# A decoder layer on one core: the score maxima of each batch element packed into one transposed block, and the decay matrix of the last two batch pairs, not only the last, built on TensorE

## The reference

```python
# 1: attention with 16 heads of 8 features, with a gate tau per query and a term delta per key
Q, K = projections of x through a linear map and a convolution of 3 taps;  V = linear(x)
scores = (Q K^T / sqrt(8)) * tau + delta
x = layernorm(x + linear(softmax(scores) V))
# 2: mLSTM cell, 4 heads of 32 features, causal
F = cumsum(log_sigmoid(fg));  log_D[s,t] = F[s] - F[t] + ig[t] for t <= s, else -inf
m = max_t log_D;  C = (q k^T / sqrt(32)) * exp(log_D - m)
hst = C / (max(|sum C|, exp(-m)) + 1e-6) @ v;  per-head normalisation
x = layernorm(x + hst)
# 3: x and the weight rounded to an fp6 grid in blocks of 32 with a scale each, matmul, bias
x = layernorm(x + xd @ wd^T + bias)
```

## Time and profile before

| | us |
|---|---|
| median of 3 runs | 238.55 (237.43 to 240.87) |
| profiled execution | 238.0 |
| its span, first to last instruction | 236.3 |
| granted TensorE clock, mean | 0.949 of 2.4 GHz |

### The profile page before, as it was taken

One profiled execution on the slowest core, in us unless ns is written; L12 is line 12 of the kernel. 1 busy time (PEld: TensorE's weight loads), 2 busy tenths in 40 slices (PEclk: granted clock), 3 DMA queues, 4 the chain that ended last, 5 costly groups with the idle time before them and its releaser, 6 DMA issues. The chain is left out here.

```text
span 236.3 us, 5909 instructions
## 1 busy us (share of the span) xinstructions
PE 208.4 (88%) x2217; PEld 132.0 (56%) x2217; DVE 154.1 (65%) x354; ACT 134.2 (57%) x346; POOL 132.0 (56%) x239
## 2 busy tenths in 40 slices
PE   1799889699999999899888899789889969699895
PEld 1676454244566455566546567366648756276552
DVE  4587889959444553557647779966684475556871
ACT  2632867556854643673763768757776465515332
POOL 7994629691232192581695848862781757523520
PEclk9997999979999999999999999999997967899799
DMA  5822110000000000202002003003002003000001
GB/s 145 206 37 78 47 47 0 1 0 3 0 3 3 0 3 1 92 3 81 11 1 94 3 1 115 0 25 97 23 0 67 28 8 103 3 22 1 22 1 47
DMA packets 10220, 8.40 MB, mean 36 GB/s; under 512 B 1872, under 2 KB 9264, under 8 KB 10192
## 3 DMA queue, kind: packets, MB, share of 16 engines
q1 hardware_dynamic: 8816, 7.83, 11.2%
q0 software_dynamic: 512, 0.18, 0.7%
q10 hardware_dynamic: 864, 0.01, 0.2%
HBM read 6.94 MB, written 1.08 MB: 34 GB/s over the span
## 5 line engine op out<-in xcount | busy, mean ns | idle before, releaser
L996 DVE TENSOR_REDUCE nm<-score 128x8 f32<-128x1024 f32 x32 | 39.1, 1223 | 22.0 <-PE score L740 22.0
L511 ACT ACTIVATE prob<-score 128x1024 f32<-128x1024 f32 x32 | 32.6, 1021 | 21.2 <-PE score L755 21.0
L740 PE MATMUL score<-km,qf 32*128 32x512 f32 x128 | 35.0, 640 | 0.8 <-ACT prob L511 0.7
L750 PE MATMUL score<-qm,kf 32*128 32x512 f32 x128 | 35.0, 639 | 0.8 <-DVE nm L996 0.8
L775 PE MATMUL pvb<-ones 128*128 128x512 bf16 x80 | 23.5, 436 | 0.0
L359 POOL CAST nmx<-nm 128x16 bf16<-128x16 f32 x16 | 4.1, 254 | 30.4 <-DVE nm L996 30.4
L381 POOL TENSOR_TENSOR u<-u,maskb 128x1024 f32<-128x1024 f32 x7 | 16.5, 2358 | 7.2 <-DMA u<-gates_out 7.2
L768 PE MATMUL pvb<-prob,vz 128*32 128x128 f32 x512 | 17.4, 277 | 2.2 <-ACT prob L511 2.2
L859 PEld LDWEIGHTS qkb<-ctm,cc 128*128 128x128 f32 x128 | 15.3, 194 | 4.3 <-issue 2.2
L768 PE MATMUL pvb<-prob,ez 128*32 128x128 f32 x512 | 16.9, 273 | 0.0
L859 PE MATMUL qkb<-ctm,cc 128*128 128x33 f32 x128 | 15.7, 278 | 1.3 <-DVE cc L1069 0.8
(11 more groups left out here) (248 smaller groups left out, 485.8 us busy)
## 6 DMA issues: line engine op xcount, KB each, us to landing
u<-gates_out SPq DMA_DIRECT2D x7, 512.0 KB, 3.7
xt<-in_x_dram SPq DMA_DIRECT2D x4, 256.0 KB, 4.3
cin<-in_ctx_dram SPq DMA_DIRECT2D x4, 256.0 KB, 3.4
out_dram<-th SPq DMA_DIRECT2D x8, 128.0 KB, 1.9
ck<-in_L_attn_convk_w_dram SPq DMA_DIRECT2D x1, 192.0 KB, 3.6
cq<-in_L_attn_convq_w_dram SPq DMA_DIRECT2D x1, 192.0 KB, 3.9
pk<-in_L_attn_kproj_w_dram SPq DMA_DIRECT2D x1, 128.0 KB, 2.9
pq<-in_L_attn_qproj_w_dram SPq DMA_DIRECT2D x1, 128.0 KB, 3.4
```

The costliest lines, as they stand in the source:

```text
L511: nc.scalar.activation(prob[:, n % 2, 2 * h:2 * h + 2, :].rearrange("p g s -> p (g s)"), sc[:, 1024 * h:1024 * (h + 1)], ACT.Exp, scale=0. ...
L740: ins = mm(sc[:, 512 * q:512 * (q + 1)], qf[r, n, :], km[r, n % (2 * CB)].rearrange("p j s -> p (j s)"), start=True, stop=True)
L750: mm(sc[:, 512 * q:512 * (q + 1)], kf[r, m, :], qm[r, m % (2 * CB)].rearrange("p j s -> p (j s)"), start=True, stop=False)
L996: nc.vector.tensor_reduce(nm[:, n % RING, 8 * h:8 * (h + 1)], sc[:, 1024 * h:1024 * (h + 1)].rearrange("p (h s) -> p h s", h=8), AX_X, ALU ...
```

## The change

- `nmx` is one block of 128 columns per element: column 32 g + 4 s + j holds part s of the maximum of head 4 g + j. One transpose instead of four, and `nmT` is 128 x 128. POOL's split has the same four instructions.
- Since the four j now share their columns, the right one must be picked: new tensors `msel` and `sel`, made once on DVE in step `vzero`. `sel[:, j, :]` is one in the rows whose index is j modulo 4. Form B adds the maxima with 8 matmuls of 32 x 128 columns (j outside, the two banks of the half inside) instead of 2 of 32 x 512.
- `LATE` is 6: pairs 6 and 7 have their decay matrix built on PE and their row-wise steps on DVE; the `dec_done` counts follow, and `x2b` on POOL, with the late steps' indices, comes twice.
- `warm` issues one matmul per step, 80 steps.
- `PLACES` is new throughout.

The diff, cut to its core:

```diff
-LATE = PAIRS - 1
+LATE = PAIRS - 2
...
-        mcol = sb("mcol", [P, J]);
+        mcol = sb("mcol", [P, J]); msel = sb("msel", [P, J]); sel = sb("sel", [P, J, P], BF16)
...
-        nmx = sb("nmx", [P, RING, J * (S + 1)], BF16)
-        nmT = sb("nmT", [P, RING, J * S], BF16)
+        nmx = sb("nmx", [P, RING, P], BF16)
+        nmT = sb("nmT", [P, RING, S], BF16)
...
-                    x3 = nmx[:, n % RING, :].rearrange("p (j c) -> p j c", j=J)
-                    hi, mid, lo = (x3[:, :, J * s:J * s + 3 * 32 + 1:32] for s in range(3))
+                    x3 = nmx[:, n % RING, :].rearrange("p (g c) -> p g c", g=G)
+                    hi, mid, lo = (x3[:, :, J * s:J * (s + 1)] for s in range(3))
...
-                    nc.scalar.activation(nmT[:, n % RING, :], trb[:, 0:J * S // 2].bitcast(BF16), ACT.Copy).then_inc(nmT_sb, 1)
+                    nc.scalar.activation(nmT[:, n % RING, :], trb[:, 0:S // 2].bitcast(BF16), ACT.Copy).then_inc(nmT_sb, 1)
...
                         pe.wait_ge(nmT_sb, m + 1)
-                        for q in (2 - 2 * h, 3 - 2 * h):
-                            r = slice(32 * q, 32 * (q + 1))
-                            ins = mm(sc[:, 512 * q:512 * (q + 1)], ones[r, :], nmT[r, m % RING, :], start=False, stop=True)
+                        if k == 0:
+                            pe.wait_ge(vzero, 1)
+                        for j in range(J):
+                            for q in (2 - 2 * h, 3 - 2 * h):
+                                r = slice(32 * q, 32 * (q + 1))
+                                ins = mm(sc[:, 512 * q + S * j:512 * q + S * (j + 1)], sel[r, j, :], nmT[r, m % RING, :], start=False, stop=(j == J - 1))
                         ins.then_inc(b_ready, 1)
...
                     pe.wait_ge(*pved)
-                    for k in range(2):
-                        mm(pvb[:], ones[:], ones[:].unsqueeze(1).to_broadcast([P, 512 // P, P]), start=True, stop=True)
+                    mm(pvb[:], ones[:], ones[:].unsqueeze(1).to_broadcast([P, 512 // P, P]), start=True, stop=True)
...
-                    for j in range(J):
-                        ins = nc.tensor.transpose(trb[:, 0:J * S // 2].bitcast(BF16)[:, S * j:S * (j + 1)],
-                                                  nmx[:, n % RING, S * j:S * (j + 1)], identb[:])
-                    ins.then_inc(nmT_ps, 1)
+                    nc.tensor.transpose(trb[:, 0:S // 2].bitcast(BF16), nmx[:, n % RING, :], identb[:]).then_inc(nmT_ps, 1)
...
-                    nc.vector.memset(vz[:], 0.0).then_inc(vzero, 1)
+                    nc.vector.memset(vz[:], 0.0)
+                    link(nc.vector.tensor_reduce(msel[:], ident[:].rearrange("p (a j) -> p j a", j=J), AX_X, ALU.max))
+                    nc.vector.tensor_copy(sel[:], msel[:].unsqueeze(2).to_broadcast([P, J, P])).then_inc(vzero, 1)
...
-                    dve.wait_ge(dec_done, p + 1)
+                    dve.wait_ge(dec_done, p + 1 + max(0, p - LATE))
...
-                                dve.wait_ge(dec_done, p + 2)
+                                dve.wait_ge(dec_done, 2 * p + 2 - LATE)
```

More of the change, by code:

```diff
@@ L40 @@
 PHASES = 2 * (B + LAG) + 1
-LATE = PAIRS - 1
+LATE = PAIRS - 2
 PLACES = {
[10 rows of a table removed]
[L55 to L62, removed]
[7 rows of a table removed]
[L70 to L75, removed]
[6 rows of a table removed]
-    "mkk": (0, 1, 2, 3, 17, 18, 19, 23, 36, 37, 40, 41, 49, 51, 52, 53), "res": (4, 5, 6, 12),
-    "mkq": (7, 8, 10, 11, 14, 15, 20, 22, 38, 39, 42, 43, 57, 58, 59, 60), "gcb": (9, 13, 21, 24, 26, 27, 31, 32),
[3 rows of a table removed]
-    "out": (75, 81, 85, 96, 102, 107, 110), "x2b": (109,), "spread": (0, 1, 2, 3, 6, 8, 9),
-    "store": (4, 5, 7, 10, 11, 12, 13, 14),
[11 rows of a table added]
+    "hst": (84, 94, 123, 131, 159, 171, 195, 215), "xdT": (96, 118, 137, 146, 190, 197, 223, 251),
+    "ffn": (99, 126, 141, 150, 194, 211, 227, 255),
+    "warm": (175, 176, 178, 179, 180, 181, 183, 184, 185, 186, 188, 189, 191, 192, 193, 198, 199, 200, 201, 202, 203, 204, 205, 206, 207, 208, 209, 210, 212, 213, 214, 216, 217, 218, 219, 220, 221, 222, 224, 225, 226, 228, 229, 230, 231, 232, 233, 234, 235, 236, 237, 238, 239, 240, 241, 242, 243, 244, 245, 246, 247, 248, 249, 250, 252, 253, 254, 256, 257, 258, 259, 260, 261, 262, 263, 264, 265, 266, 267, 268),
+    "vzero": (0,), "wab_o": (1,), "tapt": (2, 4, 15, 16, 30, 31, 37, 40), "wm_o": (3, 5), "ww_o": (6, 12),
+    "tapd": (7, 11, 17, 18, 27, 28, 35, 36), "wt_o": (8,), "wd": (9,), "fb": (10,), "bias": (13,),
+    "ko": (14, 21, 33, 39), "qo": (19, 23, 34, 41), "wo_o": (20,), "qs": (22, 32, 38, 44), "wr_o": (24,),
+    "max": (25, 29, 42, 43, 46, 48, 49, 51, 54, 56, 59, 62, 65, 67, 73, 77, 81, 87, 89, 93, 98, 103, 105, 107, 114, 120, 123, 127, 130, 136, 137, 147),
[8 rows of a table added]
+    "idt": (1, 2, 11, 12, 27, 29, 39, 41), "idd": (3, 4, 14, 16, 23, 25, 37, 38),
+    "get": (5, 6, 17, 18, 32, 33, 44, 45), "ged": (8, 10, 20, 21, 26, 30, 40, 43), "cxe": (9, 49, 56, 63),
+    "th": (13, 31, 42, 47), "dt": (15, 22, 36, 46), "cme": (24, 28, 51, 54, 57, 60, 71, 74),
+    "nmTe": (34, 52, 58, 65, 73, 79, 86, 97, 106, 114, 120, 127, 140, 147, 157, 164), "edx": (48,),
+    "exps": (50, 53, 55, 59, 62, 64, 69, 72, 77, 78, 83, 88, 92, 93, 102, 105, 110, 111, 117, 119, 122, 130, 136, 139, 143, 146, 150, 152, 162, 166, 167, 172),
[6 rows of a table added]
+    "mkk": (0, 1, 2, 3, 4, 6, 7, 15, 32, 33, 35, 36, 55, 56, 57, 59),
+    "mkq": (5, 11, 13, 14, 18, 19, 20, 21, 39, 40, 41, 43, 61, 62, 65, 66), "res": (8, 9, 10, 22),
+    "gcb": (12, 16, 26, 27, 29, 30, 38, 42),
[3 rows of a table added]
+    "x2b": (103, 105), "spread": (0, 1, 3, 4, 6, 8), "store": (2, 5, 7, 9, 10, 11, 12, 13),
@@ L354, in _ @@
                         pool.wait_ge(nmT_ps, n - RING + 1)
-                    v = nm[:, n % RING, :].rearrange("p (g j) -> p j g", j=J)
-                    rv = nr[:].rearrange("p (j g) -> p j g", j=J)
-                    x3 = nmx[:, n % RING, :].rearrange("p (j c) -> p j c", j=J)
-                    hi, mid, lo = (x3[:, :, J * s:J * s + 3 * 32 + 1:32] for s in range(3))
+                    v = nm[:, n % RING, :].rearrange("p (g j) -> p g j", j=J)
+                    rv = nr[:].rearrange("p (g j) -> p g j", j=J)
+                    x3 = nmx[:, n % RING, :].rearrange("p (g c) -> p g c", g=G)
+                    hi, mid, lo = (x3[:, :, J * s:J * (s + 1)] for s in range(3))
                     link(nc.gpsimd.tensor_copy(hi, v))
@@ L406, in _ @@
                     nc.gpsimd.tensor_tensor(x2b[:], x2[:], fbc[:].unsqueeze(1).to_broadcast([P, 2, D]), ALU.add).then_inc(x2b_done, 1)
-                if due("x2b", t) is not None:
-                    pool.wait_ge(x2_done, LATE + 1)
-                    pool.wait_ge(z3_done, LATE)
+                if (i := due("x2b", t)) is not None:
+                    p = LATE + i
+                    pool.wait_ge(x2_done, p + 1)
+                    pool.wait_ge(z3_done, p)
                     nc.gpsimd.tensor_tensor(x2b[:], x2[:], fbc[:].unsqueeze(1).to_broadcast([P, 2, D]), ALU.add).then_inc(x2b_done, 1)
@@ L1094, in _ @@
                                             ALU.mult).then_inc(t2_done, 1)
-                if due("z2l", t) is not None:
-                    dve.wait_ge(t2_done, LATE + 1)
-                    hf = hc[:, LATE % 2].rearrange("p (b h) d -> p b (h d)", b=2)
+                if (i := due("z2l", t)) is not None:
+                    p = LATE + i
+                    dve.wait_ge(t2_done, p + 1)
+                    hf = hc[:, p % 2].rearrange("p (b h) d -> p b (h d)", b=2)
                     link(nc.vector.tensor_tensor(hf, hf, rows[:, 0, :].unsqueeze(1).to_broadcast([P, 2, D]), ALU.mult))
-                    dve.wait_ge(x2_done, LATE)
-                    nc.vector.tensor_tensor(z2[:], hf, x1[:, LATE % 3, :, 0:D], ALU.add).then_inc(z2_done, 1)
-                if due("x2l", t) is not None:
-                    dve.wait_ge(rs2_done, LATE + 1)
-                    dve.wait_ge(qa_done, LATE)
+                    dve.wait_ge(x2_done, p)
+                    nc.vector.tensor_tensor(z2[:], hf, x1[:, p % 3, :, 0:D], ALU.add).then_inc(z2_done, 1)
+                if (i := due("x2l", t)) is not None:
+                    p = LATE + i
+                    dve.wait_ge(rs2_done, p + 1)
+                    dve.wait_ge(qa_done, p)
                     for v in range(2):
@@ L1106, in _ @@
                     ins.then_inc(x2_done, 1)
-                if due("xdl", t) is not None:
-                    dve.wait_ge(qa_done, LATE + 1)
-                    dve.wait_ge(xdT_ps, LATE)
+                if (i := due("xdl", t)) is not None:
+                    p = LATE + i
+                    dve.wait_ge(qa_done, p + 1)
+                    dve.wait_ge(xdT_ps, p)
                     fold = "p b (k e) -> p (b k) e"
@@ L1112, in _ @@
                                             qs8[:, 1].unsqueeze(2).to_broadcast([P, 2 * D // QB, QB]), ALU.mult).then_inc(xd_done, 1)
```

(9 more changed lines are left out.)

## The result

The changed kernel took 247.8 us as the median of 4 runs (244.45 to 249.17), where the kernel before took 237.99 beside it (237.29 to 240.87). The ratio is 1.033, with a 95% interval of 1.019 to 1.047: slower, where 232.7 us was forecast. The same kernel run once more gave 1.018 (1.007 to 1.030). So the change costs some 2 to 3%; that it costs anything is clear of the noise, that it costs over 2% is not. Medians are of all executions, while single executions that the chip disturbed are left out of all ratios.

The account below looks back on a forecast made before the run. TensorE's matmuls were taken to bound the score part, and step order the tail. Score end 185.0 plus tail 45.4 gave a 230.4 us span, 232.7 as a median (2.5% less); range 228.5 to 241.

Parts of the forecast that it names:

- So the last score half ends at 183.9 + 2.5 - 2.7 + 1.3 = 185.0 us: Score part: old end, plus steps moved in from the tail, less saved transposes, plus the new maxima matmuls.
- bounds plus and minus 2 us, taken as nothing, since the same matmuls remain: Head: all `k` and `q` projections come ahead of score step 3; this reordering was priced at zero.
- +1.3 us: Score part: cost of adding maxima by 8 small matmuls instead of 2, +0.04 us a half over 32 halves.
- Both rivals on it (0.62 and 0.87 us): Maxima matmuls: row groups don't overlap (239.1 us, chance 0.08), or each also waits for its load (247.1, 0.12).
- the 0.14 for slower: Whole kernel: chance of a slower result, 0.12 from matmuls waiting for loads plus 0.02 of the second rival.
- the bare chain of 43.9: Tail from the last score half: sum of step durations without half clock or waits for POOL, against 52.4 us before.
- The 1.5 us that I added for half clock: Tail: allowance for fillers and DVE steps up to `hst7`, raising the tail to 45.4 us.
- the first rival: Tail gains more, with fillers at full clock: 229 to 231 us, or 226.5 if score idle shrinks; chance 0.15.
- The stalls of a new order in the score part: Score part: waits opened by the reordering, said to give the second rival's time, 238 to 240 us.
- the second rival: Tail: `qk6` and 16 fillers at half clock delay pair 7's gate sums; 238 to 240 us, chance 0.25.
- It is wrong if the score part ends past 190: Score part: sign against the forecast, whose last score half was to end at 185.0 us.

Follow-up runs that it names:

- block_only: Kernel before with the one-block maxima alone, its own order of steps; 238.09 us against 238.49, ratio 0.994.
- old_all_late6: Changed kernel with the old order of steps up to `y17`, the new order behind it, pair 6 on TensorE, no fillers; 235.66 us, ratio 0.985 to before.
- before_filled: Kernel before plus 45 filler matmuls in TensorE's waits; 237.47 us against 238.13 for the kernel before.
- new_filled: Changed kernel plus 13 filler matmuls, which nobody reads, in four of TensorE's waits; 239.66 us against 238.85 for the kernel before.
- new_filled_head: Changed kernel plus 44 fillers in the score part and three ahead of `wab`, `wm` and `ww` in the head; 235.54 us, ratio 0.989 to before.
- old_late6_filled_head: One-block maxima, pair 6 on TensorE, old order up to `y17`, 45 fillers plus two ahead of `wab` and `wm`; 230.18 us against 238.13 for before.
- best: `old_late6_filled_head` with one more filler, ahead of `ww` in the head; 231.35 us against 238.59 for the kernel before, ratio 0.969.

## Why the prediction was wrong

**The step that failed** is "So the last score half ends at 183.9 + 2.5 - 2.7 + 1.3 = 185.0 us", and in it the sentence on the order: "bounds plus and minus 2 us, taken as nothing, since the same matmuls remain". The last half was written at 201.8 us, 16.8 later. The matmuls did remain; their clock, the waits between them and the side of the first Exp on which some of them stand did not. By cause, up to the last Exp:

| | us |
|---|---|
| clock not granted in the score part | +8.3 |
| more waits of TensorE in the score part | +5.9 |
| less work in the score part | -4.4 |
| head: order +3.2, half speed up to about 25 us +4.0 | +7.2 |
| sum: last Exp ends at 202.92 instead of 185.93 | +17.0 |

*Work.* Before has two projections of k between its score steps, as single rows:

```profile
79.24 2.84 PE L669 MATMUL trb<-xTp,wT 128*128 128x512 f32 x6
...
87.35 2.84 PE L669 MATMUL trb<-xTp,wT 128*128 128x512 f32 x6
```

After has them before the first form B. I had read that move and priced it at nothing. It takes 5.7 us of work out of a part where it filled TensorE's time and puts it ahead of the first Exp. Others moved the other way: ten matmuls of `ce` and four of `tc`, 2.4 us. Their rows in the score part, before and then after, and `eT`, which only before has there:

```profile
L726 PE MATMUL yb<-cen,cT 128*128 128x136 f32 x10 | 1.8, 295 | 0.0
L715 PE MATMUL yb<-ident,cin 128*128 128x128 f32 x4 | 0.6, 272 | 0.0
L707 PE MATMUL trb<-ident,edt 128*128 128x128 f32 x4 | 0.7, 286 | 0.0
```
```profile
L727 PE MATMUL yb<-cen,cT 128*128 128x136 f32 x20 | 3.5, 298 | 0.0
L716 PE MATMUL yb<-ident,cin 128*128 128x128 f32 x8 | 1.3, 279 | 0.0
```

That is 4.0 us less in the score part. With the transposes (-2.7), the new form (+0.3), `ffn3` (+0.5) and `F6` (+0.4) it should hold some 5.5 us less; 4.4 is what the rows give, and the difference is not resolved. The `hst4` and `xdT3` of my sum count in neither difference, since both kernels run them before the last Exp ends.

*Head.* `block_only` splits its 7.2 us. It has the head order of before, and its TensorE, like that of after, ran at half speed up to about 24 us (5.13 us for the first projection of k):

```profile
0.00:65.88 65.88, 54.23 (x259) 31.86 (x259) 47.19 (x91) 35.45 (x68) 40.90 (x78) 0.97 0.20 51
```

Its first Exp ends 4.0 us later than before's: that is speed. After's ends another 3.2 us later: that is order, the work moved across the first Exp. Idle time in the heads of before and after is the same (61.84 - 51.35 and 69.05 - 58.54, both 10.5 us). That the new order brings the late rise of the speed is not shown. TensorE takes its steps up to `ww0` in the same order in both kernels, and the speeds already differ there: the first six matmuls of that step with one column each take 0.87 us in before and 1.28 in after. The rise is late in all six traces with the new head and no fillers in it, but also in three of seven with the old head (`block_only`, `old_all_late6`, `before_filled`). So up to 4.0 us of the loss in this trace may be luck of the execution. Fillers ahead of three early steps brought the first Exp 3.2 us forward in the changed kernel (69.24 to 66.02).

*Clock of the scores.* I took it as full, since before shows 0.99. This was a state of the old order and not of the stage. `new_filled` shows that waits below 1 us each, close together, brought the half clock. The Trainium skill ("TensorE: Matmul & The Clock Gate", Part 1) says that the throttled state is the default and that activity releases it. The traces agree: 0.74 behind the three waits, 1.00 with the same waits filled.

*Waits.* The longest sums of TensorE's waits in the score part of after:

```profile
PE pvb L772 <- ACT prob L512: 3.5, 5, 1.1
PE score L741 <- ACT prob L512: 3.0, 6, 0.6
PE score L741 <- DVE cc L1064: 1.8, 3, 0.9
```

In before the first of these is 2.2 us and the second 0.7. The new order asks for Exps and for `c` earlier than they are there. Which of its many moved steps do it was not tried one by one and stays open; that it is the order and not the clock is shown by `new_filled_head`, whose score part at a clock of 0.99 is idle for 5.4 us more than the old order's.

**The new form of the maxima.** 0.42 us a half was forecast, 0.39 measured, so +1.3 us was really +0.3; the transposes gave about their 2.7, by the 2.5 of `block_only`. Both rivals on it (0.62 and 0.87 us) are out. They held 0.20 of my chances, and 0.12 of the 0.14 for slower. By the 81 ns of the Trainium skill ("TensorE: Matmul & The Clock Gate", Back-to-back issue gap) an estimate is 0.79 us, and the row does not bear it out for matmuls of alternating row groups. The prediction counted the transposes for the overlap of different row groups; they use all rows and say nothing of that, and only the new form's row does.

**`sel` and `msel`** took 0.68 us inside a wait of VectorE. Nothing, as forecast.

**The tail**, from the last score half on, was forecast 7 us shorter and is 11.5 shorter (40.9 against 52.4 us), 3 us less than even the bare chain of 43.9. `hst7` starts 24.6 us behind the last score half (226.42 - 201.8) where 27 were forecast for the bare chain:

```profile
218.98 0.73 PE L840 MATMUL score<-x1T,cT 32*128 32x128 f32 x16
...
225.33 0.61 PE L873 MATMUL yb<-wdC,xdT 128*128 128x128 f32 x4
225.77 0.81 PE L778 MATMUL pvb<-ones 128*128 128x512 bf16 x3
226.42 1.87 PE L859 MATMUL qkb<-ctm,cc 128*128 128x33 f32 x16
```

From the end of `hst7` on it is 14.4 us for the forecast 15.0. The 1.5 us that I added for half clock was not needed, since the tail ran at 1.00. POOL's mask and add came six times, and no step of 8 elements on VectorE took over 0.70 us, as said. So the first rival, with a tail of some 42 us, was nearest, and it was worth nothing because the other end of the kernel moved.

**The rivals.** "The stalls of a new order in the score part" was there as half a sentence of the second rival, sized at 8 us or so. It was the larger part of the cause (8.3 + 5.9 us, nearly twice the size), and nothing in my list of what would be slower held it. The sentence "It is wrong if the score part ends past 190" named the right place.

## What to carry to other kernels

In a stage that one engine fills, a new order is an edit with its own price, even when every instruction stays. Count what it takes out of the stage's waits, and count the waits that it opens: here three of them, 2.35 us in all, were followed by some 10 us at half clock. When part of a change loads a full stage and part relieves a chain, try each on the old order. Here pair 6 on TensorE with the old order, one-block maxima and fillers in the waits gave 0.969 of the time before (231.35 us). How much of it the fillers gave is less sure: the 0.985 without them is from another group of runs.

## What the runs showed of the hardware

Three TensorE waits of 0.86, 0.60 and 0.89 us within 4 us were followed by some 10 us at half clock. Thirteen filler matmuls in these and the next waits removed that and a second stretch, and brought the Exp of half 18 forward by 8 us.

What the clock is worth in a tail of small steps depends on the tail. In the kernel before, 0.93 instead of 0.86 made it no shorter (50.98 against 50.37 us). With pair 6 on TensorE, the same tail took 44.98 us at 1.00 (`old_late6_filled_head`) and 48.13 at 0.93 (`best`).

In the head of after the granted clock reads 1.00 while the matmuls take twice their later time (5.49 us for six that take 2.74 in `best`). There the durations tell the speed and the clock's row does not; the clock record of that trace has its first entry at 25.1 us (13.3 in before):

```profile
0.00:24.30 24.30, 17.10 (x53) 11.99 (x54) 14.71 (x37) 7.30 (x10) 18.30 (x45) 1.00 0.47 113
```

Row-tiled matmuls of 32 rows and 128 columns with a weight load each ran 8 in 0.39 us with 0.214 us for one, so 0.025 us apart, on two alternating row groups: their loads, 0.098 us each by the record, cost next to nothing (0.39 us for the 8 against 0.38 for the old 2).
